# A graph network kernel in which TensorE multiplies the identity matrix beside its own work in five loops

## The chip, the cores and the metric

The kernel runs on one core of a Trainium2 chip. A core has five engines that run their own instruction streams and meet through semaphores: TensorE (matmul), VectorE, ScalarE, GpSimd (here it issues indirect DMAs) and SyncE (here it issues direct DMAs). The metric is the device time of one execution in microseconds (us).

## What is computed

Four graph networks are applied one after the other to 100000 nodes of 32 features, over 50000 edges (`src`, `dst`), each with a layer norm ahead of it and a residual:

```python
edge_index = jnp.stack([src, dst])
h = jnp.maximum(_layernorm(x, axis=-1), 0.0)
x = x + _L0_gnn_ref(h, edge_index, ...)          # softmax aggregation and an MLP
h = jnp.maximum(_layernorm(x, axis=-1), 0.0)
x = x + _L1_gnn_ref(h, ..., edge_index)          # edge MLP with batch norm
h = jnp.maximum(_layernorm(x, axis=-1), 0.0)
x = x + _L2_gnn_ref(h, edge_index, edge_attr_3, ...)
h = jnp.maximum(_layernorm(x, axis=-1), 0.0)
x = x + _L3_gnn_ref(h, edge_attr_8, ..., edge_index)
```

The change lies in the last two. `_L2_gnn_ref` is two spline convolutions, `_L3_gnn_ref` three message passing layers:

```python
# L2, twice
xW = jnp.einsum('ni,kio->nko', x, weight)
for s in range(S):
    msg = msg + basis[:, s, None] * xW[src, wi[:, s]]
out = segment_sum(msg, dst) / jnp.clip(deg, 1.0)[:, None]
h = jax.nn.elu(out + x @ root + bias)
# L3, three times
e = edge_attr @ We[l] + be[l]
msg = jax.nn.relu(x[src] + e)
h = x + segment_sum(msg, dst)
x = jax.nn.leaky_relu(h @ W[l] + b[l], negative_slope=0.01)
```

## The kernel before

Edges are sorted by destination and lie as 128 partitions x 392 columns. A stage walks over them in 49 chunks (`NCH`) of 8 columns (`CH`), that is 1024 edges, and all of a stage's loops are written out, but for those of the last stage, which are hardware loops over two chunks at a time. Nothing schedules: the order on an engine is the order in which its function issues. In each stage the engines form a pipeline over chunks.

Each stage has its own set of buffers and begins and ends with a barrier of all engines. The last part of the program, stage by stage:

- `all_nodes` works on all nodes (not over chunks).
- `conv1_edges`, the first spline stage (names `c_`): GpSimd gathers rows of nodes (8 transfers a chunk of `B.other`; in 17 of the 49 chunks 8 more of `B.own`), VectorE normalises and widens them into `c_hz` (line 1443), TensorE transposes `c_hz` in 8 pieces into two PSUM banks (line 1478), ScalarE copies these to `c_hzT` (line 1499), TensorE multiplies with the spline weights (line 1489, four products `psU` a chunk, two of them a chunk later), and VectorE weighs and sums these (lines 1453 and 1460). VectorE's third product of a chunk, `times(2)`, waits for a `psU` that stands on TensorE behind the transposes of the next chunk.
- `conv2_edges`, the first convolution: the same with gathers from a table of sums. Not changed.
- `conv3_edges`, the second convolution's end (names `c_` too): TensorE turns the features (`Turned.turn`, line 1615) and the edge attributes (`EdgeTerm.turn`, line 1759), ScalarE copies them, TensorE multiplies by `root` (line 1632) and by the edge weights (line 1772), VectorE adds the gathered sums (line 1875), applies elu, residual and norm. ScalarE copies the next chunk's transposes only after this chunk's square (`ahead(c + 1)`).
- `gin_edges`, layer 3, called for l = 0 and 1 (names `g_`): VectorE sums (line 1985), TensorE turns and multiplies, with a bias row of ones first (line 1630), ScalarE copies the result (line 1973), VectorE applies leaky relu.
- `last_edges`, the last stage (names `out_`): VectorE sums (line 2076), TensorE transposes twice (line 2058), ScalarE copies, TensorE multiplies (lines 2063, bias, and 2065, weights), ScalarE copies (line 2049), VectorE makes rows (line 2084), GpSimd scatters them, 8 transfers a chunk (line 2035).
- Between them `close_segments` runs a scan over all edges and stores a table.

GpSimd may run at most three chunks ahead of VectorE in the gathering stages (three buffers, `NR = 3`), and two behind it in the last.

Of the kernel before, what the change touches and what calls it, by code (L numbers as in the profile page):

```python
# [11 lines left out]
P = 128  # L12
# [211 lines left out]
FAKE = 100000  # L224
TOP = 3.0e38
G2, Q4 = 2, SF // P
GQ = G2 * Q4


# [1272 lines left out]
def conv1_edges(g, B, W2, W01, M, S, QB):  # L1502

    N2, NR = 2 * CH, 3
    with Phase(g, "c1") as ph:
# [5 lines left out]
        ring = [ph.sb(f"ring{i}", [P, N2, D + 1]) for i in range(NR)]  # L1511
        hd = ph.sb2("hd", [P, CH, D])
        sp_ = Spline(ph, g, W2, W01, M, 2)
        early = chosen(g, g.EARLY)
        loaded = [ph.sem(f"loaded{i}") for i in range(NR)]
        landed = [16 * CH if c in early else 16 * N2 for c in range(g.NCH)]
# [45 lines left out]
        @block.tensor  # L1562
        def _(pe):
            for c in range(g.NCH):
                sp_.turn(pe, c, 0)
                sp_.turn(pe, c, 1)
                if c:
                    sp_.multiply(pe, c - 1, (2, 3), g.spline[0])
                sp_.multiply(pe, c, (0, 1), g.spline[0])
            sp_.multiply(pe, g.NCH - 1, (2, 3), g.spline[0])  # L1570

        @block.vector
# [210 lines left out]
def conv3_edges(g, B, rows_b, M, S, QB, table):  # L1783

    N2, NR = 2 * CH, 3
    with Phase(g, "c3") as ph:
# [8 lines left out]
        x3, xc, sq = ph.sb2("x3", [P, N2, D]), ph.sb2("xc", [P, N2, D]), ph.sb("sq", [P, N2, D])  # L1795
        s, var, sd, rs = (ph.sb(n, [P, N2]) for n in ("s", "var", "sd", "rs"))
        yd, mm = ph.sb2("yd", [P, CH, D]), ph.sb("mm", [P, CH, D])
        tn, et = Turned(ph, g), EdgeTerm(ph, g, rows_b)
        block = ph.block()

        @block.gpsimd
# [36 lines left out]
        @block.tensor  # L1838
        def _(pe):
            for c in range(g.NCH):  # L1840
                pe.wait_ge(dgot[c % NR], 16 * (c // NR + 1))
                tn.turn(pe, c, halves_of(S, din[c % NR], c))
                et.turn(pe, c)
                tn.multiply(pe, c, g.root[1])
                et.multiply(pe, c, 0)

        @block.scalar
        def _(act):
# [72 lines left out]
def gin_edges(g, B, rows_b, M, S, QB, table, l):  # L1921

    N2, NR = 2 * CH, 3
    with Phase(g, f"g{l}") as ph:
        lk, summed, copied, new = ph.sem("lk"), ph.sem("summed"), ph.sem("copied"), ph.sem("new")
        got, dgot = [ph.sem(f"got{i}") for i in range(NR)], [ph.sem(f"dgot{i}") for i in range(NR)]
        kept = ph.sem2("kept")
        ring = [ph.sb(f"ring{i}", [P, CH, D]) for i in range(NR)]
        din = [ph.sb(f"din{i}", [P, CH, D]) for i in range(NR)]
        agg, e = ph.sb2("agg", [P, N2, D]), ph.sb2("e", [P, N2, D])  # L1930
        yd, mm = ph.sb2("yd", [P, CH, D]), ph.sb("mm", [P, CH, D])
        tn, et = Turned(ph, g), EdgeTerm(ph, g, rows_b)
        block = ph.block()

        @block.gpsimd
        def _(pool):
            for c in range(g.NCH):
                if c >= NR:
                    pool.wait_ge(summed, c - NR + 1)
                gather_from(g, pool, table, QB, ring[c % NR], c, 0, got[c % NR])  # L1940

        @block.sync
        def _(sp):
            def load(c):
                if c >= NR:
                    sp.wait_ge(summed, c - NR + 1)
                sp.dma_start(din[c % NR][:, :, :], lin(g, g.dst_lin, c)).then_inc(dgot[c % NR], 16)

            def store(c):
                sp.wait_ge(new, c + 1)  # L1950
                sp.dma_start(lin(g, g.dst_lin, c), yd[c % 2][:, :, :]).then_inc(kept[c % 2], 16)
            load_ahead(g, sp, NR, load, store)
            for i in range(2):
                sp.wait_ge(kept[i], 16 * ((g.NCH + 1 - i) // 2))

        @block.tensor
        def _(pe):
            for c in range(g.NCH):
                et.turn(pe, c)
                pe.wait_ge(summed, c + 1)  # L1960
                tn.turn(pe, c, [agg[c % 2][:, 4 * q:4 * q + 4, :] for q in range(4)])
                et.multiply(pe, c, l + 1)
                tn.multiply(pe, c, g.w3[l], g.bias[:, 5 + l, :])

        @block.scalar
        def _(act):
            for c in range(g.NCH):
                et.flatten(act, c)
                tn.flatten(act, c)
                act.wait_ge(tn.done, c + 1)  # L1970
                if c >= 2:
                    act.wait_ge(new, c - 1)
                act.copy(e[c % 2][:, :, :], tn.psD[c % 2][:, :].rearrange("p (t f) -> p t f", f=D)).then_inc(tn.used, 1)  # L1973

        @block.vector
        def _(v):
            link = Link(v, lk)
            for c in range(g.NCH + 1):
                if c < g.NCH:
                    cols = slice(c * CH, (c + 1) * CH)  # L1980
                    v.wait_ge(got[c % NR], 16 * CH * (c // NR + 1))
                    v.wait_ge(dgot[c % NR], 16 * (c // NR + 1))
                    if c >= 2:
                        v.wait_ge(tn.turned, c - 1)
                    link.inc(v.tensor_tensor(agg[c % 2][:, 0:CH, :], S[:, cols, :], ring[c % NR][:, :, :], ALU.add))
                    link(v.tensor_tensor(agg[c % 2][:, CH:N2, :], M[:, cols, :], din[c % NR][:, :, :], ALU.add))
                    v.sem_inc(summed, 1)
                if c:
                    k = c - 1
                    cols, b = slice(k * CH, c * CH), k % 2  # L1990
                    v.wait_ge(tn.used, c)
                    if k >= 2:
                        v.wait_ge(kept[b], 16 * (k // 2))
                    link(v.scalar_tensor_tensor(S[:, cols, :], e[b][:, 0:CH, :], 0.01, e[b][:, 0:CH, :], ALU.mult, ALU.max))  # L1994
                    v.scalar_tensor_tensor(yd[b][:, :, :], e[b][:, CH:N2, :], 0.01, e[b][:, CH:N2, :], ALU.mult, ALU.max).then_inc(new, 1)
                    et.message(v, link, k, S, M, mm)
# [7 lines left out]
def last_edges(g, B, M, out):  # L2004

    N, W = g.N, g.W
    with Phase(g, "out") as ph:
# [5 lines left out]
        agg, aT, y = ph.sb("agg", [P, CH, D]), ph.sb("aT", [P, 256]), ph.sb("y", [P, CH, D])  # L2013
        rowr, idxr = ph.sb2("rowr", [P, CH, D]), ph.sb2("idxr", [P, CH], I32)
        psA, psD = ph.ps("psA"), ph.ps("psD")
        block = ph.block()

        @block.sync
# [34 lines left out]
        def _(pe):  # L2053
            def body(k, b, first):
                c = 2 * k + b
                pe.wait_ge(zin, c + 1)
                for q in range(2):
                    ins = pe.transpose(psA[:, q * P:(q + 1) * P], agg[:, 4 * q:4 * q + 4, :].rearrange("p t f -> p (t f)"), g.ident[:, :])  # L2058
                ins.then_inc(turned, 1)
                pe.wait_ge(flat, c + 1)  # L2060
                if not (first and b == 0):
                    pe.wait_ge(leaky, c)
                pe.matmul(psD[:, 0:256], g.ones[0:1, :], over(g.bias[:, 7, :], 1, CH), start=True, stop=False, skip_group_check=True)  # L2063
                for q in range(2):
                    ins = pe.matmul(psD[:, q * P:(q + 1) * P], aT[:, q * P:(q + 1) * P], g.w3[2][:, :], start=False, stop=False, skip_group_check=True)  # L2065
                ins.then_inc(done, 1)
            chunks(g, pe, body)

        @block.vector
# [374 lines left out]
```

## Time and profile before

| | us |
|---|---|
| median of 3 runs | 9387.17 |
| lowest and highest run | 9379.37, 9951.77 |
| the profiled execution | 9400.52 |
| its span, first to last instruction | 9398.8 |
| busy in the span: TensorE matmul, weight load | 2821.1, 1768.9 |
| busy in the span: VectorE, ScalarE, GpSimd | 4174.4, 1297.4, 5190.7 |
| mean granted TensorE clock, share of full | 0.608 |

In the rows further down PE is TensorE's matmul, PEld its weight load, DVE VectorE, ACT ScalarE, POOL GpSimd. A row of the timeline has the start in the span, the time, the engine, the line in the kernel, the operation, what it writes and reads, the shape (partitions x elements), the count of instructions merged into it, and in brackets how long the engine was idle before and what ended that. Ends of matmuls are modelled. A granted clock of 0.50 is 1.2 GHz, of 1.00 2.4 GHz.

### The profile page before, as it was taken

What the parts mean: (1) busy time and instruction counts of PE and PEld (TensorE: products, weight loads), DVE (VectorE), ACT (ScalarE), POOL (GpSimd) and SP (SyncE); (2) the same over time, 40 slices, a digit from 0 to 9 for tenths busy, and PEclk for the clock granted to TensorE, in tenths of its full rate; (3) what the DMA queues carried; (4) which work ended last, traced back from release to release, by engine and by line L of the source; (5) the groups of instructions that cost most, each with busy time, mean ns of one, the idle gap of its engine ahead of it and who ended that gap; (6) DMA issues with size and microseconds to landing.
All of it is one profiled execution on the core that took longest, in us unless ns stands there. A gap on an engine that the chain in (4) does not pass through costs nothing. (4 is left out here: it accounts for less than half of the span.)

```text
span 9398.8 us, 39754 instructions
## 1 busy us (share of the span) xinstructions
PE 2821.1 (30%) x8711; PEld 1768.9 (19%) x8711; DVE 4174.4 (44%) x7182; ACT 1297.4 (14%) x2213; POOL 5190.7 (55%) x5107
## 2 busy tenths in 40 slices
PE   0000000000232310127663444277333144245222
PEld 0000000000231100003221333155222123123111
DVE  4367448970024440104543677677655411312311
ACT  0000001000011110016551000011033111011000
POOL 5744741887436637770335665266266366366366
PEclk9965555555555555558876666677655555555555
DMA  1100100001133201111111111122134222222111
GB/s 41 26 20 16 25 15 6 19 18 36 44 102 48 38 16 23 21 16 33 41 38 34 33 35 34 41 32 32 46 64 66 59 33 34 48 31 35 51 31 28
DMA packets 364620, 331.83 MB, mean 35 GB/s; under 512 B 115499, under 2 KB 339968, under 8 KB 363379
## 3 DMA queue, kind: packets, MB, share of 16 engines
q0 software_dynamic: 163072, 77.69, 9.5%
q1 hardware_dynamic: 199282, 249.37, 8.1%
q10 hardware_dynamic: 2048, 2.41, 0.1%
q8 instruction: 70, 1.15, 0.1%
q14 instruction: 148, 1.21, 0.0%
HBM read 173.11 MB, written 158.67 MB: 35 GB/s over the span
## 5 line engine op out<-in xcount | busy, mean ns | idle before, releaser
L917 POOL DMA_INDIRECT c_ring<-tab,QB x784 | 758.7, 968 | 732.2 <-POOLq L102 306.6
L917 POOL DMA_INDIRECT g_ring<-tab,QB x784 | 749.7, 956 | 621.3 <-issue 234.4
L917 POOL DMA_INDIRECT l_ring<-in_x_dram,a_own x392 | 528.6, 1348 | 386.9 <-POOLq L102 267.7
L1489 PE MATMUL c_psU<-spline,c_hzT 96*128 96x288 f32 x1568 | 547.8, 497 | 190.8 <-DVE c_V L1453 145.2
L917 POOL DMA_INDIRECT l_ring<-agg_tab,QA x392 | 393.5, 1004 | 363.3 <-POOLq L102 205.6
L917 POOL DMA_INDIRECT nodes_ring<-nodes,b_own x256 | 254.1, 993 | 594.7 <-DMA x2d_lin<-nodes_ring 516.6
L917 POOL DMA_INDIRECT H<-xe_tab,idx_a x392 | 402.1, 1026 | 320.9 <-DVEq L788 200.6
L2035 POOL DMA_INDIRECT out_dram<-out_rowr,out_idxr x392 | 386.4, 986 | 284.7 <-DVE out_idxr L2079 149.1
L917 POOL DMA_INDIRECT c_ring<-nodes,b_other x392 | 397.7, 1015 | 262.5 <-DVEq L1586 137.8
L1366 POOL DMA_INDIRECT nodes<-l1s_rowr,a_out x392 | 386.2, 985 | 264.7 <-DVE l1s_rowr L1382 145.5
L917 POOL DMA_INDIRECT sort_ring<-in_x_dram,sort_raw x392 | 402.3, 1026 | 121.3 <-issue 120.3
L917 POOL DMA_INDIRECT rows_b<-b_edges,idx_b x392 | 393.4, 1004 | 134.4 <-issue 122.8
L1994 DVE SCALAR_TENSOR_TENSOR S<-g_e 128x256 f32<-128x256 f32 x98 | 41.8, 426 | 922.7 <-ACT g_e L1973 580.3
L1453 DVE TENSOR_TENSOR c_V<-c_psU,W 128x576 f32<-128x576 f32 x392 | 286.8, 751 | 359.3 <-DMA out_dram<-nodes_o 149.2
L1460 DVE TENSOR_REDUCE M<-c_V 128x64 f32<-128x576 f32 x392 | 432.9, 1124 | 0.0
L1489 PEld LDWEIGHTS c_psU<-spline,c_hzT 96*128 96x128 f32 x1568 | 350.3, 240 | 356.8 <-issue 223.1
L1632 PE MATMUL c_psD<-root,c_aT 128*128 128x128 f32 x784 | 196.1, 429 | 526.8 <-issue 345.0
L1478 PE MATMUL c_psT<-ident,c_hz 128*96 128x128 f32 x784 | 192.7, 411 | 385.2 <-DVE c_hz L1443 292.1
L273 PE MATMUL sort_psC<-ident,sort_x 98*128 98x98 f32 (+1 forms) x148 | 30.3, 381 | 881.9 <-issue 555.1
L1632 PEld LDWEIGHTS c_psD<-root,c_aT 128*128 128x128 f32 x784 | 168.0, 316 | 567.4 <-issue 361.8
L298 DVE TENSOR_TENSOR sort_x<-sort_x 98x512 f32<-98x512 f32 (+1 forms) x315 | 189.6, 602 | 156.8 <-remote 62.1
L1630 PE MATMUL g_psD<-bias,ones 1*128 1x512 f32 x196 | 188.6, 1060 | 189.3 <-issue 188.2
(473 smaller groups left out, 8052.4 us busy)
## 6 DMA issues: line engine op xcount, KB each, us to landing
tab<-M SPq DMA_DIRECT2D x5, 6272.0 KB
nodes<-l_xout SPq DMA_DIRECT2D x40, 322.3 KB
nodes_x<-nodes SPq DMA_DIRECT2D x50, 257.8 KB
c_din<-dst_lin SPq DMA_DIRECT2D x98, 128.0 KB
c_ring<-tab,QB POOLq DMA_INDIRECT x784
dst_lin<-c_yd SPq DMA_DIRECT2D x98, 128.0 KB
g_din<-dst_lin SPq DMA_DIRECT2D x98, 128.0 KB
g_ring<-tab,QB POOLq DMA_INDIRECT x784
```

The costliest lines, as they stand in the source:

```text
L273: ins = pe.transpose(dst[:, i, 0:n], src[0:n, i // Q4, (i % Q4) * P:(i % Q4 + 1) * P], self.g.ident[0:n, 0:n])
L298: link.inc(v.tensor_tensor(lo, x, y, ALU.min))
L917: pool.indirect_dma_start(out=ring[:, at + j, :], out_offset=None, in_=table, in_offset=bass.IndirectOffsetOnAxis(ap=idx[:, w:w + 1], axis ...
L1366: pool.indirect_dma_start(out=g.nodes2, out_offset=bass.IndirectOffsetOnAxis(ap=A.out[:, w:w + 1], axis=0), in_=rowr[k % NR][:, j, :], in_ ...
L1453: v.tensor_tensor(self.V[n % 3][:, :, :, :], self.psU[i % 2][:, :, 0:288].rearrange("p t (j o) -> p t j o", o=D), over(self.W01[:, at:at + ...
L1460: v.tensor_reduce(self.M[:, at:at + 2, :], self.V[n % 3][:, :, :, :].rearrange("p t j o -> p t o j"), AX.X, ALU.add).then_inc(self.added, 1)
L1478: ins = pe.transpose(self.psT[n % self.nT][0:3 * D, t * P:(t + 1) * P], self.hz[c % 2][:, 4 * u + t, :, :].rearrange("p k f -> p (k f)"), ...
L1489: ins = pe.matmul(self.psU[i % 2][:, t, 0:288], self.hzT[c % 2][:, (2 * i + t) * P:(2 * i + t + 1) * P], w[:, :, :].rearrange("p j o -> p ...
L1630: pe.matmul(o[:, :], g.ones[0:1, :], over(bias, 1, 2 * CH), start=True, stop=False, skip_group_check=True)
L1632: ins = pe.matmul(o[:, q * P:(q + 1) * P], self.aT[c % 2][:, q * P:(q + 1) * P], w[:, :], start=bias is None, stop=bias is None, skip_grou ...
L1994: link(v.scalar_tensor_tensor(S[:, cols, :], e[b][:, 0:CH, :], 0.01, e[b][:, 0:CH, :], ALU.mult, ALU.max))
L2035: pool.indirect_dma_start(out=out, out_offset=bass.IndirectOffsetOnAxis(ap=idxr[b][:, j:j + 1], axis=0), in_=rowr[b][:, j, :], in_offset=N ...
```

## The change

A class `Spare` gives TensorE matmuls of the 128x128 identity with the identity repeated to 512 columns, into a PSUM bank of their own that nothing reads. They carry no wait and signal nothing. Per chunk there are 4 + 7 in the first spline stage, 6 + 7 in the second convolution, 5 + 6 in layer 3 (both calls), 14 in the last stage. What the kernel computes is untouched.

```diff
+class Spare:
+    def __init__(self, g, ps):
+        self.g, self.ps = g, ps
+        self.n = ps.shape[1] // P
+
+    def run(self, pe, n):
+        for i in range(n):
+            pe.matmul(self.ps.rearrange("p (t f) -> p t f", f=P), self.g.ident[:, :], over(self.g.ident[:, :], 1, self.n),
+                      start=True, stop=True)
...
@@ conv1_edges
+        spare = Spare(g, ph.ps("spare")[:, :])
...
             for c in range(g.NCH):
                 sp_.turn(pe, c, 0)
                 sp_.turn(pe, c, 1)
+                spare.run(pe, 4)
                 if c:
                     sp_.multiply(pe, c - 1, (2, 3), g.spline[0])
                 sp_.multiply(pe, c, (0, 1), g.spline[0])
+                spare.run(pe, 7)
             sp_.multiply(pe, g.NCH - 1, (2, 3), g.spline[0])
...
@@ conv3_edges
                 tn.turn(pe, c, halves_of(S, din[c % NR], c))
                 et.turn(pe, c)
+                spare.run(pe, 6)
                 tn.multiply(pe, c, g.root[1])
                 et.multiply(pe, c, 0)
+                spare.run(pe, 7)
...
@@ gin_edges
                 et.turn(pe, c)
+                spare.run(pe, 5)
                 pe.wait_ge(summed, c + 1)
                 tn.turn(pe, c, [agg[c % 2][:, 4 * q:4 * q + 4, :] for q in range(4)])
                 et.multiply(pe, c, l + 1)
                 tn.multiply(pe, c, g.w3[l], g.bias[:, 5 + l, :])
+                spare.run(pe, 6)
...
@@ last_edges
                 ins.then_inc(done, 1)
+                spare.run(pe, 14)
             chunks(g, pe, body)
```

TensorE's order in the first spline stage, at its second and third chunk, before (a call of matmul a count; `c_psT` are the transposes, `c_psU` the products; a call of line 1489 is 128x288):

```order
L1478 MATMUL c_psT<-ident,c_hz 96x128 x8
L1489 MATMUL c_psU<-spline,c_hzT 128x288 x8
L1478 MATMUL c_psT<-ident,c_hz 96x128 x8
L1489 MATMUL c_psU<-spline,c_hzT 128x288 x8
L1478 MATMUL c_psT<-ident,c_hz 96x128 x8
```

and after (line numbers are those of the changed kernel):

```order
L1493 MATMUL c_psT<-ident,c_hz 96x128 x8
L238 MATMUL c_spare<-ident 128x512 x4
L1504 MATMUL c_psU<-spline,c_hzT 128x288 x8
L238 MATMUL c_spare<-ident 128x512 x7
L1493 MATMUL c_psT<-ident,c_hz 96x128 x8
```

Between a chunk's transposes and its products now stand 4 spares, and 7 before the next transposes.

TensorE's order in the last stage's hardware loop, before, one chunk and the start of the next (`out_psA` are the transposes, `out_psD` the products):

```order
L2058 MATMUL out_psA<-ident,out_agg 128x128
L2063 MATMUL out_psD<-bias,ones 128x256 [waits sort_back,prep_mlp1]
L2065 MATMUL out_psD<-w_2,out_aT 128x128 x2
L2056 REGISTER_ALU
L2058 MATMUL out_psA<-ident,out_agg 128x128 [waits prep_blank]
```

and after:

```order
L2081 MATMUL out_psA<-ident,out_agg 128x128
L2086 MATMUL out_psD<-bias,ones 128x256 [waits sort_back,prep_mlp1]
L2088 MATMUL out_psD<-w_2,out_aT 128x128 x2
L238 MATMUL out_spare<-ident 128x512 x14
L2079 REGISTER_ALU
L2081 MATMUL out_psA<-ident,out_agg 128x128 [waits prep_blank]
```

The 14 spares stand between a chunk's products and the next chunk's transposes. (Names of semaphores in brackets are those under which their numbers were first used.)

## Rows read from the trace of the kernel before

**Rows 1.** Stretches: us; busy us (count) of PE, PEld, DVE, ACT, POOL; clock; DMA.
```profile
5050.00:5900.00 850.00, 388.38 (x1164) 264.11 (x1164) 574.43 (x872) 71.92 (x147) 518.80 (x514) 0.65 0.17 34
6772.00:7372.00 600.00, 193.37 (x735) 159.61 (x735) 309.76 (x681) 231.10 (x339) 378.39 (x392) 0.56 0.39 65
7453.00:8060.00 607.00, 284.50 (x833) 171.54 (x833) 110.38 (x294) 65.94 (x147) 375.25 (x392) 0.55 0.24 32
8164.00:8745.00 581.00, 273.41 (x809) 165.12 (x809) 107.36 (x286) 64.34 (x143) 355.22 (x372) 0.56 0.24 32
8824.00:9392.00 568.00, 149.68 (x392) 83.87 (x392) 66.09 (x196) 36.50 (x98) 386.32 (x392) 0.50 0.12 31
```

**Rows 2.** First and last start of one instruction a chunk, by line, in four stages.
```profile
L1443 DVE TENSOR_TENSOR c_hz<-S,W x49: 957/957/959, 5058.0 to 5893.1; 128x768 f32<-128x768 f32 x49
L1875 DVE TENSOR_TENSOR c_agg<-c_psD,c_ring x49: 424/424/426, 6784.0 to 7365.0; 128x256 f32<-128x256 f32 x49
L1985 DVE TENSOR_TENSOR g_agg<-S,g_ring x49: 424/426/493, 7465.2 to 8049.6; 128x256 f32<-128x256 f32 x49
L2076 DVE TENSOR_TENSOR out_agg<-M,out_din x49: 417/420/427, 8824.2 to 9363.3; 128x256 f32<-128x256 f32 x49
```

**Rows 3.** Timeline (start us, us, what) and clock: weight loads before 512-column passes.
```profile
4034.66 0.34 PEld L2215 LDWEIGHTS nodes_ps<-nodes_hT,w 128*128 128x128 f32 x1 [0.52 <-issue]
4035.51 0.34 PEld L2215 LDWEIGHTS nodes_ps<-nodes_hT,w 128*128 128x128 f32 x1 [0.52 <-issue]
...
4037.15 0.19 PEld L2215 LDWEIGHTS nodes_ps<-nodes_hT,w 128*128 128x128 f32 x1 [0.44 <-issue]
4037.58 0.19 PEld L2215 LDWEIGHTS nodes_ps<-nodes_hT,w 128*128 128x128 f32 x1 [0.24 <-issue]
...
4030.00:4036.50 6.50, 5.42 (x7) 2.32 (x8) 3.18 (x5) 2.55 (x5) 4.97 (x6) 0.50 0.09 5
4036.50:4044.00 7.50, 3.22 (x7) 0.88 (x5) 0.69 (x1) 0.69 (x1) 5.72 (x6) 0.96 0.08 5
```

**Rows 4.** Timeline: TensorE at one place of two chunks in a row, layer 3.
```profile
7718.82 0.42 PE L1759 MATMUL g_psX<-ident,rows_b 128*104 128x128 f32 x1
...
7722.81 0.27 PE L1759 MATMUL g_psX<-ident,rows_b 128*104 128x128 f32 x1
```

**Rows 5.** Timeline: the last stage's two transposes of a chunk.
```profile
9062.36 0.69 PE L2058 MATMUL out_psA<-ident,out_agg 128*128 128x128 f32 x2 [11.74 <-DVE out_agg L2076]
```

**Rows 6.** Timeline, last stage: TensorE's product and ScalarE's copy, twice.
```profile
9064.66 1.22 PE L2065 MATMUL out_psD<-w,out_aT 128*128 128x128 f32 x4
...
9065.99 0.37 ACT L2049 COPY out_r<-out_psD 128x256 f32<-128x256 f32 x1 [2.53 <-PE out_psD L2065]
...
9100.54 1.22 PE L2065 MATMUL out_psD<-w,out_aT 128*128 128x128 f32 x4
...
9114.52 0.37 ACT L2049 COPY out_r<-out_psD 128x256 f32<-128x256 f32 x1 [15.18 <-DMA g_ring<-tab,QB]
```

**Rows 7.** Timeline of GpSimd in the first convolution's loop.
```profile
6251.90 1.16 POOL L917 DMA_INDIRECT c_ring<-tab,QB  x1 [2.65 <-DVEq L1733]
...
6266.45 0.95 POOL L917 DMA_INDIRECT c_ring<-tab,QB  x1 [0.31 <-issue]
6267.70 0.95 POOL L917 DMA_INDIRECT c_ring<-tab,QB  x1 [0.30 <-issue]
```

**Rows 8.** Timeline of TensorE in one chunk, second convolution.
```profile
7071.22 2.08 PE L1632 MATMUL c_psD<-root,c_aT 128*128 128x128 f32 x8 [11.04 <-issue]
...
7074.79 0.34 PE L1759 MATMUL c_psX<-ident,rows_b 128*104 128x128 f32 x1
```

**Rows 9.** Timeline of VectorE, first spline stage: widening, first late product, next widening.
```profile
5514.47 0.96 DVE L1443 TENSOR_TENSOR c_hz<-S,W 128x768 f32<-128x768 f32 x1
...
5519.38 0.76 DVE L1453 TENSOR_TENSOR c_V<-c_psU,W 128x576 f32<-128x576 f32 x1 [1.57 <-PE c_psU L1489]
...
5528.80 0.96 DVE L1443 TENSOR_TENSOR c_hz<-S,W 128x768 f32<-128x768 f32 x1
```

More of the change, by code:

```diff
@@ L1797, in conv3_edges @@
         yd, mm = ph.sb2("yd", [P, CH, D]), ph.sb("mm", [P, CH, D])
-        tn, et = Turned(ph, g), EdgeTerm(ph, g, rows_b)
+        tn, et, spare = Turned(ph, g), EdgeTerm(ph, g, rows_b), Spare(g, ph.ps("spare")[:, :])
         block = ph.block()
@@ L1931, in gin_edges @@
         yd, mm = ph.sb2("yd", [P, CH, D]), ph.sb("mm", [P, CH, D])
-        tn, et = Turned(ph, g), EdgeTerm(ph, g, rows_b)
+        tn, et, spare = Turned(ph, g), EdgeTerm(ph, g, rows_b), Spare(g, ph.ps("spare")[:, :])
         block = ph.block()
@@ L2015, in last_edges @@
         psA, psD = ph.ps("psA"), ph.ps("psD")
+        spare = Spare(g, ph.ps("spare")[:, :])
         block = ph.block()
```

## The prediction

> **What bounds the kernel now.** I read the page first: over the span no engine is busy for more than about half the time, so shares decide nothing, and each changed stage is read by itself. The table of stretches [rows 1] shows the five changed loops over the 49 chunks of edges: the first spline stage, the second convolution, the two runs of layer 3, and the last stage. The reader is to see there that GpSimd's 8 gathers or scatters of each chunk fill about 0.61 to 0.68 of each stage, and TensorE 0.26 to 0.47 at a granted clock of 0.50 to 0.65 of full, the last stage wholly at 0.50, which is the 1.2 GHz level.
>
> A GpSimd transfer starts every 1.25 us [rows 7], so 8 need 10.0 us. The first and last chunk of each stage [rows 2] give the time of one chunk (48 steps between 49 chunks): first spline stage (5893.1-5058.0)/48 = 17.4 us, second convolution (7365.0-6784.0)/48 = 12.1, layer 3 (8049.6-7465.2)/48 = 12.2 (its second run, alike in [rows 1], is taken as equal), last stage (9363.3-8824.2)/48 = 11.2. So in the last four GpSimd is nearly the bound, 1 to 2 us short of it.
>
> The rest is a late hand-over from TensorE. [rows 6] show it: the four matmuls of line 2065 that begin at 9064.66 end 1.22 us later, and ScalarE starts at 9065.99, at once. Those at 9100.54 end at 9101.76 and ScalarE starts at 9114.52, 12.8 us late, while GpSimd issued one scatter after the other; it had to stop for it only now and then. In the first convolution, which is not changed, VectorE paces the loop and GpSimd rests 2.65 us before its next 8 gathers [rows 7]; there I found nothing late once the first chunks were through. I don't know the cause. What I use is only this: a chunk time over about 12.6 us gives GpSimd such rests, so a stage paced by TensorE should be free of most late hand-overs.
>
> **The change, priced.** One `spare` is a plain 128x128 by 128x512 matmul in f32. The nearest rows are the same shape in the stage over all nodes: there weight loads, one a 512-column pass, begin 0.85 us apart at clock 0.50 (4034.66, 4035.51) and 0.43 us apart at 0.96 (4037.15, 4037.58) [rows 3]. A plain f32 matmul is two such passes: in [rows 6] two calls of line 2065 stand as x4, and in [rows 5] two transposes as x2. So one spare is 0.86 us at the full clock and 1.71 at half. Both ends: 11 spares are 9.4 to 18.8 us, 13 are 11.2 to 22.2, 14 are 12.0 to 23.9. At the upper end TensorE would have no idle time at all in a chunk of 11 to 17 us, and [rows 3] show that a run of matmuls without a rest takes it to the upper level; I therefore take the full clock, 2.4 GHz, for all of them. The Trainium skill, page TensorE: Matmul & The Clock Gate, section Why this matters for your kernels, says to leave no longer idle gaps between bursts of matmuls, since the clock drops to half after one; by that rule alone the change would be a gain (the trace agrees on the two paces).
>
> They can be free only where they fit in TensorE's rest. They stand in program order, so everything behind them on TensorE waits.
>
> *Last stage.* Nothing of the next chunk passes the 14 spares. TensorE's own work runs from the transposes at 9062.36 over the hand-over to ScalarE to line 2065 at 9064.66 and its four passes of 0.21 [rows 5, 6]: 3.15 us at half clock. At full clock the passes lose about 1.1 of it (half of 0.43 + 0.85 + 0.85); I take 2.0. 2.0 + 12.0 = 14.0 us a chunk against 11.2: 48 x 2.8 = **+133 us**. Bounds: 13.0 (no wait between) gives +86, 15.2 gives +190.
>
> *Layer 3, twice.* Own work of a chunk from line 1759 at 7718.82 to the same line at 7722.81 [rows 4]: 4.0 us, in which the clock rose; fully at the upper level about 3.6. With 9.4: 13.0 us against 12.2, 48 x 0.8 = 40. At the start GpSimd may issue three chunks, 30 us, without a rest, a time in which hand-overs are late now too; now the chain catches up with chunks of 4 to 6 us, later it can't. I add 20. **+60 us each, +120.** Bounds +20 and +90 each.
>
> *Second convolution.* From line 1632 at 7071.22 to line 1759 at 7074.79 plus one pass [rows 8]: 3.8 us at half clock, about 2.0 at full. The wait for ScalarE's copy lies under the 6 spares. 2.0 + 11.2 = 13.2 against 12.1: 48 x 1.1 = 53, and 7 for the start: **+60 us**. Bounds +30 and +90.
>
> *First spline stage.* Here VectorE's loop counts. It widens at 5514.47, waits for the product until 5519.38 (4.9 us), and widens again at 5528.80 [rows 9]: 14.3 us a chunk where nothing is late; the mean of 17.4 comes from chunks with 16 gathers and late hand-overs. Four spares now stand between the transposes and that product: +3.4. At the full clock the 8 transposes and 4 passes lose 0.9 + 0.9, so the wait ends 1.7 later: 16.0 us. The other 7 spares (6.0 us) end before the next widening: 0.9 transposes + 3.4 + 16 passes of 0.25 (4.0) + 6.0 = 14.3 of 16.0. If all late hand-overs stay, 17.4 + 1.7: +80. If all go: 48 x (16.0-17.4) = -67. As GpSimd now rests more, but still has chunks of 16, I take **-30 us**.
>
> *All else* (first convolution, the stages between, the sort, the stage over the nodes) stands as it was; a stage's last spares end under VectorE's and the stores' tail. GpSimd, SyncE, VectorE and ScalarE get no instruction, and no wait is added: the spares' bank is their own. What queues behind them on TensorE is its next transposes and products, and ScalarE's copies and VectorE's sums wait for those.
>
> Sum: -30 + 60 + 120 + 133 = **+283 us**, on the profiled span of 9398.8 (9400.5 with what lies around it); the median of the runs is 9387, 0.14% below, so 9387 + 283 = **9670 us**, +3.0%.
>
> **Rivals.**
>
> *Evened out (0.13).* Paced by TensorE, the late hand-overs vanish in all stages and the waits between spares are shorter than I take: -67, +30, 2 x 20, +86 make +89: 9476 us. For it: the regular chunks of [rows 7]. Against: the last stage alone is above its present pace by pure passes.
>
> *The warm clock wins (0.06), on the other side.* The spares fit in the rest, TensorE's own work runs at double clock, and hand-overs come on time. TensorE is busy 388 + 193 + 285 + 273 + 150 = 1289 us in the five stages [rows 1]; at 0.5 to 0.65 a full clock would save some 500, of it perhaps half on the path: -250, 9137 us. It decides if 11 to 14 spares take less than the rest of a chunk: that needs a spare to be one pass, 0.43 us (14 = 6.0 us beside 2.0 in 11.2). The x4 for two calls speaks against it. The rule of the Trainium skill cited above (TensorE: Matmul & The Clock Gate) points this way.
>
> *Late in every chunk (0.19).* The spares' passes meet the same slowness: between 9100.54 and 9114.52 four passes took 14.0 us, and the 22 to 28 added a chunk are queued ahead of the hand-overs. If each chunk of the last four stages loses 3 us more to it, 4 x 48 x 3 = 576 more: 10246 us; with 1 us, 9862. GpSimd's rest of 3 us a chunk speaks against, as it does in the first convolution; runs of 16 gathers in the first spline stage for it.
>
> **How the numbers follow.** My forecast has 0.62, its own range 9575 to 9780 by the bounds of its terms. The range to hold 8 in 10 runs from 9500, inside the evened-out case, to 9950, inside the late one. A measurement here can tell 2% (188 us) from no change: slower means over 9575. Slower: 0.60 of the forecast, and 0.19 of the last, and a little of the evened-out case, 0.82; same 0.13; faster 0.05.
>
> **What would show it.** In the profile after, the spare line should stand with 2 x (49 x 11 + 49 x 13 + 2 x 49 x 11 + 49 x 14) = 5880 passes of 0.43 us pitch, the granted clock near 1.0 in the five stages, the last stage's chunks 14.0 us apart, layer 3's 13.0, the second convolution's 13.2 and the first spline stage's about 16.5, and GpSimd resting 3 to 4 us after each 8. The forecast is wrong if the clock stays near 0.5 (then the chunks would be 20 us and over, and the time over 11,000 us), if spares are single passes, or if ScalarE's copies start many microseconds after TensorE's last pass in most chunks.

## The result, and the profile after

The changed kernel takes 9851.99 us (median of 4, 9849.09 to 9863.49) where the kernel before takes 9387.17. (That is the median of three runs; a fourth, at 9951.77, was in a slower state of the chip and is left out of the ratio.) The ratio is 1.0495, with a 95% interval of 1.0474 to 1.0515: 465 us, 4.9% slower. The prediction said 9670 us, +283: right in direction, 182 us too low.

The page of the changed kernel first. The lines are its row of granted clock over 40 equal slices, and its three groups of spare passes (count | busy us, mean ns | idle before):

```profile
PEclk9975555555655655578779897776998898899999
...
L238 PE MATMUL c_spare<-ident 128*128 128x512 f32 x2352 | 1062.6, 601 | 14.2 <-issue 12.4
L238 PE MATMUL g_spare<-ident 128*128 128x512 f32 x2156 | 961.5, 597 | 0.0
...
L238 PE MATMUL out_spare<-ident 128*128 128x512 f32 x1372 | 598.7, 594 | 0.0
```

2352 + 2156 + 1372 = 5880 passes: a spare is two passes, as priced. The table of stretches of the changed kernel (the columns of [rows 1]), for the first spline stage, the second convolution, layer 3 twice and the last stage:

```profile
5039.00:5986.00 947.00, 752.34 (x2189) 399.64 (x2190) 561.34 (x857) 67.42 (x144) 524.18 (x511) 0.89 0.15 30
6888.00:7536.00 648.00, 626.67 (x1963) 322.33 (x1962) 302.83 (x666) 231.83 (x333) 374.53 (x383) 0.98 0.34 58
7637.00:8280.00 643.00, 594.70 (x1815) 287.86 (x1816) 105.29 (x282) 67.34 (x140) 361.46 (x383) 0.96 0.22 29
8399.00:9042.00 643.00, 594.17 (x1816) 287.85 (x1817) 105.97 (x285) 67.34 (x140) 361.57 (x383) 0.96 0.22 29
9151.00:9817.00 666.00, 643.79 (x1703) 297.19 (x1704) 62.26 (x191) 35.76 (x96) 370.18 (x376) 0.99 0.10 26
```

The clock, between 0.50 and 0.65 in [rows 1], is now between 0.89 and 0.99, and TensorE fills 92 to 97% of the last four stages. The first and last start of one instruction a chunk, to be set against [rows 2]; for the first spline stage I take a reduction of its normalization, of which all 49 are recorded, and show that row of the kernel before (L1582) too:

```profile
L1582 DVE TENSOR_REDUCE c_ln_s<-c_ring x49: 668/674/695, 5053.4 to 5888.5; 128x16 f32<-128x512 f32 x49
```

```profile
L1600 DVE TENSOR_REDUCE c_ln_s<-c_ring x49: 667/674/687, 5038.8 to 5985.8; 128x16 f32<-128x512 f32 x49
L1895 DVE TENSOR_TENSOR c_agg<-c_psD,c_ring x49: 424/425/427, 6887.8 to 7536.4; 128x256 f32<-128x256 f32 x49
L2007 DVE TENSOR_TENSOR g_agg<-S,g_ring x49: 425/426/427, 7636.6 to 8280.4; 128x256 f32<-128x256 f32 x49
L2007 DVE TENSOR_TENSOR g_agg<-S,g_ring x49: 424/426/427, 8398.9 to 9042.0; 128x256 f32<-128x256 f32 x49
L2100 DVE TENSOR_TENSOR out_agg<-M,out_din x49: 416/419/427, 9150.6 to 9817.2; 128x256 f32<-128x256 f32 x49
```

From these rows the 450 us between the two profiled spans (9398.8 and 9848.8) can be placed:

| where | before, us | after, us | change | forecast |
|---|---|---|---|---|
| first spline stage | 835.1 | 947.0 | +112 | -30 |
| second convolution | 581.0 | 648.6 | +68 | +60 |
| layer 3, both runs | 584.4 + 585.5 | 643.8 + 643.1 | +117 | +120 |
| last stage | 539.1 | 666.6 | +128 | +133 |
| between the stages, the end, and all ahead of the first spline stage | | | +26 | 0 |

In the last line +41 lie between the stages and at the end, of which 18 and 20 us stand behind the two runs of layer 3 (8280.4 to 8398.9 is 118.5 us, where it was 100.7), and -15 ahead of the first spline stage. Three lines of the sum hold within 8 us. One, the first spline stage, has the wrong sign.

The timeline of the first spline stage in the changed kernel shows what it waits for. The product (line 1504, 8 passes) begins at 5573.93, at full pace, and ends 2.10 us later; VectorE, which waits for it in line 1468, begins at 5584.51, 8.5 us late. ScalarE's two copies, whose transposes stand ahead of that product on TensorE, begin 4.2 us apart. GpSimd issued one transfer after the other up to 5580.65; VectorE moves 2.9 us after that one's end:

```profile
5573.93 2.10 PE L1504 MATMUL c_psU<-spline,c_hzT 96*128 96x288 f32 x8
...
5574.70 0.58 ACT L1514 COPY c_hzT<-c_psT 96x512 f32<-96x512 f32 x1 [7.26 <-DMA rows_b<-b_edges,idx_b]
...
5578.86 0.58 ACT L1514 COPY c_hzT<-c_psT 96x512 f32<-96x512 f32 x1 [3.58 <-DMA rows_b<-b_edges,idx_b]
...
5580.65 0.95 POOL L932 DMA_INDIRECT c_ring<-nodes,b_other  x1 [0.30 <-issue]
5584.51 0.76 DVE L1468 TENSOR_TENSOR c_V<-c_psU,W 128x576 f32<-128x576 f32 x1 [12.61 <-DMA out_dram<-nodes_o]
```

So the late hand-overs of [rows 6] were still there, once in every three chunks: chunks of 15.7, 17.2 and 25.1 us, 58.1 together. They had even become a little more frequent: of the stage's 48 chunks 12 took over 20 us before, and 16 do now.

### The profile page after: what moved, and what is told of

Read it like the earlier page. It is cut to its first block and busy times, and to the rows that moved or that the text cites. A ratio compares the mean times of both kernels' runs of the same rounds, so it can differ in the third digit from the quotient of the medians.

```text
span 9848.8 us, 51514 instructions
## 1 busy us (share of the span) xinstructions
PE 4866.1 (49%) x14591; PEld 2574.0 (26%) x14591; DVE 4169.0 (42%) x7182; ACT 1306.9 (13%) x2213; POOL 5200.6 (53%) x5107
## 5 line engine op out<-in xcount | busy, mean ns | idle before, releaser
L238 PE MATMUL c_spare<-ident 128*128 128x512 f32 x2352 | 1062.6, 601 | 14.2 <-issue 12.4
L238 PE MATMUL g_spare<-ident 128*128 128x512 f32 x2156 | 961.5, 597 | 0.0
L238 PE MATMUL out_spare<-ident 128*128 128x512 f32 x1372 | 598.7, 594 | 0.0
L1504 PE MATMUL c_psU<-spline,c_hzT 96*128 96x288 f32 x1568 | 490.6, 453 | 189.2 <-DVE c_V L1468 155.2
L238 PEld LDWEIGHTS c_spare<-ident 128*128 128x128 f32 x2352 | 448.8, 194 | 507.4 <-issue 496.6
L238 PEld LDWEIGHTS g_spare<-ident 128*128 128x128 f32 x2156 | 398.5, 192 | 456.1 <-issue 456.1
L1504 PEld LDWEIGHTS c_psU<-spline,c_hzT 96*128 96x128 f32 x1568 | 313.0, 212 | 358.6 <-issue 273.4
```

The source lines that it names most:

```text
L238: pe.matmul(self.ps.rearrange("p (t f) -> p t f", f=P), self.g.ident[:, :], over(self.g.ident[:, :], 1, self.n), start=True, stop=True)
L1504: ins = pe.matmul(self.psU[i % 2][:, t, 0:288], self.hzT[c % 2][:, (2 * i + t) * P:(2 * i + t + 1) * P], w[:, :, :].rearrange("p j o -> p ...
```

## Experiments

**All experiments ran later, on four chips,** and on each of them the kernel before takes 7812 to 7826 us, not 9387. Ratios are always to the kernel before on the same chip, run beside it, and what differs from the first pair is itself a finding (below).

### The first spline stage alone, and its cause

`spline_only` keeps the 4 and 7 spares of the first spline stage and drops all others:

```
                 et.turn(pe, c)
-                spare.run(pe, 6)
...
                 et.multiply(pe, c, 0)
-                spare.run(pe, 7)
...
-                spare.run(pe, 5)
...
-                spare.run(pe, 6)
...
-                spare.run(pe, 14)
```

> The 4 and 7 spares of the first spline stage alone; the other three stages as in the kernel before. In the changed kernel that stage went from 17.4 to 19.7 us a chunk (line 1600 from 5038.8 to 5985.8, against 835.1 before). Theory A (the cost belongs to the stage itself): it takes 947 us again, and the whole kernel about 9395 + 112 + 6 - 15 = 9500 us, 1.1% over before, all other stages at their times of before. Theory B (stages act on each other, so that the stages' differences don't add): the stage stays near 835 to 860 us when the later ones have no spares, and the time is within 0.4% of before.

Ratio 1.0093 (1.0063 to 1.0123). The stage took 756 us, 15.75 a chunk, not 947:

```profile
L1600 DVE TENSOR_REDUCE c_ln_s<-c_ring x49: 671/674/689, 4019.5 to 4775.6; 128x16 f32<-128x512 f32 x49
```

The expectation had both theories start from 835 us, and the stage before is 680 us where nothing is late (next section), so neither number fits. What is left of theory A is that the stage costs +76 us by itself, without any other stage's spares; with all of them in place it takes the same 756 (`after_again`, below). It does not settle what made +112 of it in the first pair.

`before_early49` and `after_early49` move the second set of 8 gathers of the remaining 17 chunks into the stage over all nodes, in the kernel before and in the changed one:

```
-    g.PICKED, g.EARLY = 24, 32
+    g.PICKED, g.EARLY = 24, 49
```

> The same move of gathers in the kernel before, without spares. Theory F: no late hand-overs, 14.3 us a chunk instead of 17.4: 686 us instead of 835; with 0 to 170 us more in the stage over the nodes the kernel takes 9245 to 9420. Theory G: 17.4 us a chunk stay, 835 us, 9395 to 9565.

> The changed kernel, with the second set of 8 gathers of all 49 chunks (not of 32) moved ahead, into the stage over all nodes: the first spline stage then has 8 gathers in every chunk. Theory F (the late hand-overs there come with GpSimd's long runs of transfers, 8 + 16 + 8): they go, and the stage takes the 16.0 us a chunk that the prediction worked out, 770 us instead of 947. Theory G (the spares' places alone give 19.7 us a chunk): it stays over 900 us. The stage over the nodes has 17 x 8 x 1.25 = 170 us more of GpSimd's work, beside pauses of GpSimd of 30 us each: 0 to 170 us longer. By F 9680 to 9850, by G 9850 to 10020.

Measured: 1.0120 (1.0090 to 1.0150) and 1.0980 (1.0950 to 1.1011). The first spline stage took 670.9 us without and 753.7 with spares:

```profile
L1582 DVE TENSOR_REDUCE c_ln_s<-c_ring x49: 666/674/690, 4100.9 to 4771.7; 128x16 f32<-128x512 f32 x49
```

```profile
L1600 DVE TENSOR_REDUCE c_ln_s<-c_ring x49: 671/674/681, 4118.6 to 4872.3; 128x16 f32<-128x512 f32 x49
```

14.0 and 15.7 us a chunk are close to theory F's 14.3 and 16.0. But `spline_only` reached 15.75 with its runs of 16 gathers in place, so the two runs don't show that the runs of gathers made hand-overs late: here nothing was late with or without them. The moved gathers cost about 106 us in the stage over the nodes (the first spline stage starts at 4100.9 in place of 3994.9).

### The same pair again, where nothing is late

> The kernel before once more, for its trace beside the runs of this call (in the runs before this one it took 7821 us, and GpSimd's 8 transfers a chunk took 10.0 us in layer 3, without a pause). Theory H (the missing 1570 us against the first trace are hand-overs from TensorE that are no longer late): the stages that GpSimd paces take 10.0 to 10.2 us a chunk, the first spline stage 14.0, the sort 1062 us instead of 1514. Theory I (everything runs quicker by one factor, as by a quicker clock): single operations such as line 1453's reduction or a gather are shorter by 17%.

> The changed kernel beside it. Where no hand-over is late, the spares meet chunks of 10.0 us: first spline stage 15.75 against 14.0 us a chunk (+85), second convolution 13.0 against 10.2 (+134), layer 3 12.55 against 10.0 twice (+245), last stage 13.9 against 10.12 (+181), ends of stages +35 to 45: 8490 to 8530 us where before takes 7821, a ratio of 1.085 to 1.09. If late hand-overs are back, the ratio is near 1.05 as in the first pair.

The kernel before took 7805 us in one run. The changed one has ratio 1.0866 (1.0835 to 1.0898), 8502 us against 7815. First and last starts in the kernel before (first spline stage, second convolution, layer 3's first run, last stage):

```profile
L1582 DVE TENSOR_REDUCE c_ln_s<-c_ring x49: 666/673/687, 3994.9 to 4674.9; 128x16 f32<-128x512 f32 x49
L1875 DVE TENSOR_TENSOR c_agg<-c_psD,c_ring x49: 423/425/426, 5540.3 to 6032.3; 128x256 f32<-128x256 f32 x49
L1985 DVE TENSOR_TENSOR g_agg<-S,g_ring x49: 424/426/427, 6132.5 to 6612.2; 128x256 f32<-128x256 f32 x49
L2076 DVE TENSOR_TENSOR out_agg<-M,out_din x49: 415/420/427, 7282.3 to 7768.2; 128x256 f32<-128x256 f32 x49
```

and the same four places in the changed kernel:

```profile
L1600 DVE TENSOR_REDUCE c_ln_s<-c_ring x49: 666/674/697, 4016.9 to 4772.5; 128x16 f32<-128x512 f32 x49
L1895 DVE TENSOR_TENSOR c_agg<-c_psD,c_ring x49: 424/425/425, 5645.1 to 6269.8; 128x256 f32<-128x256 f32 x49
L2007 DVE TENSOR_TENSOR g_agg<-S,g_ring x49: 424/425/427, 6369.8 to 6973.2; 128x256 f32<-128x256 f32 x49
L2100 DVE TENSOR_TENSOR out_agg<-M,out_din x49: 415/420/426, 7802.3 to 8469.5; 128x256 f32<-128x256 f32 x49
```

Theory H holds and I falls: operations have the durations of the first trace (424 to 427 ns for the additions above, as in [rows 2]); what is gone are waits. The timeline of the last stage in the kernel before shows it: TensorE's product at 7500.84 ends at 7502.06 and ScalarE starts at 7502.17, while GpSimd issues scatter after scatter, 1.29 us apart, without a rest. In the first trace the same sequence gave 12.8 us of delay [rows 6]:

```profile
7500.84 1.22 PE L2065 MATMUL out_psD<-w,out_aT 128*128 128x128 f32 x4
7501.07 0.98 POOL L2035 DMA_INDIRECT out_dram<-out_rowr,out_idxr  x1 [0.30 <-issue]
7502.17 0.37 ACT L2049 COPY out_r<-out_psD 128x256 f32<-128x256 f32 x1 [2.53 <-PE out_psD L2065]
7502.36 0.98 POOL L2035 DMA_INDIRECT out_dram<-out_rowr,out_idxr  x1 [0.30 <-issue]
```

Time of a chunk in us, all from such rows divided by 48; "late" is the first pair less the second:

| stage | before, first pair | after, first pair | before again | after again | late before | late after |
|---|---|---|---|---|---|---|
| first spline stage | 17.40 | 19.73 | 14.17 | 15.74 | 3.2 | 4.0 |
| second convolution | 12.10 | 13.51 | 10.25 | 13.01 | 1.9 | 0.5 |
| layer 3 (first run) | 12.18 | 13.41 | 9.99 | 12.57 | 2.2 | 0.8 |
| last stage | 11.23 | 13.89 | 10.12 | 13.90 | 1.1 | 0.0 |

This table explains the size of the result. Where nothing is late, the spares cost 48 x (1.57 + 2.76 + 2 x 2.57 + 3.78) = 636 us in the five loops, since in the last four GpSimd's 10 us a chunk are then the bound that TensorE has to stay under. In the first pair they cost 424, as TensorE's own pace gave back 212 us of late time. It gave it back wherever the loop is TensorE's, and in the first spline stage it did not. Behind the two runs of layer 3 another 19 and 18 us are lost here (6973.2 to 7091.4 in place of 6612.2 to 6711.9 for the first), as in the first pair.

What is left of late time in the changed kernel's later stages lies at their start. In the first pair the third chunk of each run of layer 3 takes 42.5 and 42.3 us, where it takes 9.7 and 10.0 on the later chip, and the first chunk of the second convolution 34.0 in place of 12.1; no later chunk of these stages is over 15.0.

### Which spares of the first spline stage cost

`spline_ahead` keeps only the 4 spares between the transposes and the product, `spline_behind` only the 7 behind it, and `all_behind` has 11 behind it; no other stage has any. The edits, in the stage's loop of the changed kernel:

```
spline_ahead:                        spline_behind:                      all_behind:
                                     -                spare.run(pe, 4)   -                spare.run(pe, 4)
-                spare.run(pe, 7)                                        -                spare.run(pe, 7)
                                                                         +                spare.run(pe, 11)
```

> Only the 4 spares between the transposes and the first product of the first spline stage. Theory J (VectorE's loop waits for that product, the others are hidden, as the prediction worked out: +3.4 for the spares, -1.7 for the quicker clock): 15.5 to 15.8 us a chunk, the whole cost of the 11, +80 us. Theory K (TensorE as a whole is the bound, 11 spares count alike): 14.3 to 14.7 us a chunk, +20 to +35 us. If the clock falls with fewer spares, the 4 cost up to 6.8: over 17 us a chunk, +145 us or more.

> Only the 7 spares behind the product. Theory J: hidden in TensorE's rest, 13.7 to 14.0 us a chunk, and the whole kernel within 15 us of before (6 spares there took 13.78). Theory K: 14.8 to 15.3 us a chunk, +40 to +60 us.

> All 11 spares of the first spline stage stand behind the product, none ahead of it; none in the other stages. So far, without late hand-overs: no spare 14.0 to 14.2 us a chunk, 7 behind 13.8, 4 ahead 17.0, 4 ahead and 7 behind 15.7. Theory J (what counts is whether VectorE waits for a product behind the spares): TensorE's own work at full clock is 4.9 us a chunk and 11 spares 9.5, 14.4 together, so 14.3 to 14.6 us a chunk, +10 to +25 us. Theory K (the number counts, not the place): 15.7 again, +75 us.

| kernel | ratio (interval) | us a chunk | clock in the stage |
|---|---|---|---|
| none | 1 | 14.17 | 0.72 |
| 4 ahead | 1.0186 (1.0160 to 1.0212) | 17.00 | 0.80 |
| 7 behind | 0.9988 (0.9976 to 1.0000) | 13.78 | 0.95 |
| 4 ahead, 7 behind | 1.0093 (1.0063 to 1.0123) | 15.75 | 0.99 |
| 11 behind | 1.0062 (1.0041 to 1.0083) | 15.13 | 0.99 |

The clock of the fourth line is from `after_again`. In VectorE's timeline, widening (the first line of each pair) and the first product that VectorE has to wait for after it, for no spares, 4 and 7, and 4 ahead alone:

```profile
4510.25 0.96 DVE L1443 TENSOR_TENSOR c_hz<-S,W 128x768 f32<-128x768 f32 x1
...
4515.17 0.76 DVE L1453 TENSOR_TENSOR c_V<-c_psU,W 128x576 f32<-128x576 f32 x1 [1.58 <-PE c_psU L1489]
```

```profile
4509.26 0.96 DVE L1458 TENSOR_TENSOR c_hz<-S,W 128x768 f32<-128x768 f32 x1
...
4515.79 0.76 DVE L1468 TENSOR_TENSOR c_V<-c_psU,W 128x576 f32<-128x576 f32 x1 [3.19 <-PE c_psU L1504]
```

```profile
4510.28 0.96 DVE L1458 TENSOR_TENSOR c_hz<-S,W 128x768 f32<-128x768 f32 x1
...
4518.19 0.76 DVE L1468 TENSOR_TENSOR c_V<-c_psU,W 128x576 f32<-128x576 f32 x1 [4.56 <-PE c_psU L1504]
```

4.9, 6.5 and 7.9 us. The prediction had 4.9 + 3.4 - 1.7 = 6.6 for the second, so theory J's mechanism stands in these three: what delays VectorE is what lies ahead of the product. But the 4 alone are dearer than all 11. The stretches of one such chunk, TensorE's rest, then transposes and first spares, then the remaining spares and products, show why:

```profile
4504.60:4511.20 6.60, 0.34 (x2) 0.00 (x0) 5.91 (x13) 0.31 (x1) 5.08 (x6) 0.70 0.14 18
4511.20:4514.40 3.20, 3.11 (x10) 2.32 (x11) 2.42 (x4) 1.16 (x2) 2.59 (x3) 0.54 0.52 127
4514.40:4521.00 6.60, 6.10 (x20) 3.39 (x19) 2.81 (x4) 0.00 (x0) 4.87 (x6) 1.00 0.13 13
```

After 6.6 us in which it did next to nothing TensorE stands at the lower level when the transposes come, and they and the first spare go at half pace. The 7 behind had kept it at the upper one. I had expected 15.5 to 15.8 there, or over 17 if the clock fell; it fell, and the chunk takes 17.0.

`all_behind` came out at 15.13, between J (14.3 to 14.6) and K (15.7). Its row for the stage gives TensorE 695 of 726 us busy:

```profile
4015.00:4741.00 726.00, 695.08 (x2180) 374.98 (x2181) 561.43 (x856) 66.03 (x144) 500.19 (x511) 0.99 0.20 39
```

TensorE is the bound. Its chunk is 11 spares, 9.5 us, and 5.7 us of its own, with waits for VectorE to free a product's buffer among them; I had counted 4.9. VectorE waits 6.0 us for its product there, not 3.3 as with 7 behind: once TensorE is the bound, spares behind a chunk's products delay the next chunk's.

### Do spares that fit pay?

`fitting` has 0 and 6, 4 and 5, 4 and 4, and 9 spares; `narrow` has all the spares of the changed kernel with 128 columns in place of 512:

```
fitting (the last stage; the other counts likewise):
-                spare.run(pe, 14)
+                spare.run(pe, 9)
narrow:
-        spare = Spare(g, ph.ps("spare")[:, :])
+        spare = Spare(g, ph.ps("spare")[:, 0:P])
```

> Fewer spares, so many that they fit into TensorE's rest by 0.86 us each: 0 and 6 in the first spline stage, 4 and 5 in the second convolution, 4 and 4 in layer 3, 9 in the last stage (own work 2.0 to 3.6 us a chunk, so 9.7 to 10.5 of 11.2 to 12.2). Theory C (the spares cost only what does not fit): within 1% of before, 9300 to 9490. Theory D (the warm clock wins where spares fit): TensorE's clock is near 0.9 in these stages, its own work and hand-overs are quicker by 1 us a chunk, and the time is 200 us or more lower, under 9200. Theory E (each spare adds to late hand-overs, also where it fits): 9600 and over.

> The changed kernel with all its spares in their places, each of 128 instead of 512 columns. Theory L (a spare costs its columns): two passes of 0.11 us at the full clock, 0.22 us each, so 2.4 us a chunk for 11 and 3.1 for 14: all but the 4 ahead of the product fit, layer 3 and the last stage stay at 10.0 to 10.2 us a chunk, and the kernel is within 1% of before. If the clock stays at the lower level in those stages, 0.43 us each: the first spline stage +1.7 a chunk, +80 us, the rest still as before. Theory M (a spare costs a fixed time for its instruction and weights): 12 us a chunk and more in layer 3, over 3% slower. Theory D (a warm clock wins): under 7700 where before takes 7820.

`fitting`: 1.0030 (1.0013 to 1.0048). `narrow`: 1.0075 (1.0058 to 1.0092). Stretches of the first spline stage, the second convolution, layer 3's first run and the last stage, for the kernel before and for `fitting`:

```profile
3995.00:4675.00 680.00, 351.12 (x1144) 249.43 (x1144) 565.36 (x858) 70.59 (x144) 503.40 (x511) 0.72 0.21 42
5542.00:6034.00 492.00, 188.03 (x715) 156.18 (x715) 303.88 (x667) 226.40 (x334) 371.34 (x382) 0.56 0.46 76
6134.00:6614.00 480.00, 297.41 (x820) 173.87 (x819) 106.92 (x287) 64.16 (x144) 359.94 (x382) 0.50 0.30 39
7283.00:7769.00 486.00, 146.95 (x386) 82.42 (x385) 64.13 (x191) 35.71 (x96) 363.61 (x371) 0.50 0.14 35
```

```profile
3996.00:4657.50 661.50, 529.45 (x1711) 301.55 (x1712) 561.88 (x858) 67.68 (x144) 498.63 (x511) 0.94 0.21 43
5530.00:6020.00 490.00, 465.79 (x1571) 243.68 (x1570) 301.48 (x661) 225.78 (x332) 371.43 (x380) 1.00 0.47 77
6120.00:6605.00 485.00, 472.78 (x1543) 233.90 (x1544) 107.20 (x286) 67.34 (x140) 365.25 (x383) 0.99 0.30 39
7315.00:7800.00 485.00, 455.03 (x1249) 209.44 (x1247) 64.48 (x190) 35.76 (x96) 366.33 (x373) 0.99 0.13 35
```

In the second convolution and the last stage the spares do fit. The clock went from 0.56 and 0.50 to 1.00 and 0.99, and from first to last chunk the stages take 493.7 us (before 492.0) and 488.2 (485.9): theory C. GpSimd's 8 transfers are the bound at about 10 us a chunk, and a quicker TensorE has nothing to give. The Trainium skill, page TensorE: Matmul & The Clock Gate, section Why this matters for your kernels, is right about the clock here and says nothing of the time of such a stage.

In layer 3 they don't quite fit. The count was made for chunks of 12.2 us, and here GpSimd's take 10.0. TensorE has no rest, and a chunk of it takes 10.3 us:

```profile
7159.80 0.27 PE L1776 MATMUL g_psX<-ident,rows_b 128*104 128x128 f32 x1
...
7170.10 0.27 PE L1776 MATMUL g_psX<-ident,rows_b 128*104 128x128 f32 x1
```

The stage as VectorE sees it grows by only 4 us, from 480 to 484, since TensorE falls behind it: ScalarE's last copy of a product comes 18.4 us after VectorE's last addition, where it was 6.9. That is paid behind each of the two runs, 11.5 and 11.4 us. With 8 us within the runs, and against 18.6 us won in the first spline stage, it is more than half of the 21 us by which `fitting` is longer (spans of 7825.1 and 7803.6).

In `narrow` the second convolution, layer 3 and the last stage stayed at 10.2, 10.0 and 10.1 us a chunk, with the clock between 0.74 and 0.79, and only the first spline stage grew, to 15.3. There VectorE's wait for the product is 5.6 to 6.6 us in place of 4.9, by the four narrow spares ahead of it: theory L, with 1.1 us a chunk between the 0.9 and 1.7 that it allows. Theory E, on late hand-overs, could not be tested where none is late. A spare costs its columns.

### A version a little faster than both

In `spline_behind` VectorE's first product came 3.3 us after the widening in the median, instead of 4.9, and still the stage fell only by 18 us, to 661.5. The trace before has 528 gathers in that stage, 660 us at 1.25. `behind_early38` moves 6 more sets of 8 gathers out of it:

```
                 sp_.turn(pe, c, 1)
-                spare.run(pe, 4)
...
-    g.PICKED, g.EARLY = 24, 32
+    g.PICKED, g.EARLY = 24, 38
```

with the 7 behind kept and no spares elsewhere.

> The 7 spares behind the product alone took 661.5 us in the first spline stage, and 528 gathers at 1.25 us are 660: GpSimd had become its bound, while single chunks there already showed 12.5 us. Here 6 more chunks have their second 8 gathers moved into the stage over the nodes, 480 gathers stay, 600 us. Theory N (the warm clock's gain was hidden by GpSimd): the stage falls to 600 to 615 us, 65 to 80 under before; the stage over the nodes grows by 6 x 6.2 = 37 us (17 chunks cost 106 there), and the kernel is 0.3 to 0.6% faster than before. Theory O (VectorE's own loop takes 13.8 with the warm clock): the stage stays at 655 to 665 us, and the kernel is 0.2 to 0.5% slower than before.

Ratio 0.9945 (0.9926 to 0.9963), 7781 us against 7812; the stage took 614 us, as theory N has it:

```profile
L1599 DVE TENSOR_REDUCE c_ln_s<-c_ring x49: 667/677/701, 4033.9 to 4648.0; 128x16 f32<-128x512 f32 x49
```

It is 0.5% faster than the kernel before, a small gain, but the interval leaves out 1. The moved gathers alone don't give it: with all 17 sets moved and no spares the stage still took 670.9 us (`before_early49`). It was run only where nothing is late.

## Why the prediction came out as it did

- **A spare is two passes of 0.43 us, 0.86 together.** Right: 5880 passes, and the last stage's 28 lie between 9506.98 and the next chunk's transposes at 9519.00, 0.43 us each (timeline of TensorE in the changed kernel):

```profile
9504.96 0.38 PE L2081 MATMUL out_psA<-ident,out_agg 128*128 128x128 f32 x2
...
9506.98 12.18 PE L238 MATMUL out_spare<-ident 128*128 128x512 f32 x28
9519.00 0.38 PE L2081 MATMUL out_psA<-ident,out_agg 128*128 128x128 f32 x2
```

- **Last stage, 2.0 + 12.0 = 14.0 us a chunk, +133.** Right: 13.9 in both pairs, and +128 in the first.
- **Layer 3, 13.0 a chunk and 20 us for the start, +60 each.** Right in the stage, +59 and +58, and for the reason given: chunks take 12.9 us once the start is over, and the third, 42.5 us where it was 35.8 before, is no longer caught up. The stage's end was priced at nothing, and 18 and 20 us more lie behind it: VectorE's last addition no longer marks the end of TensorE's work. In the second run it starts at 9042.0, and ScalarE's last copy of a product (line 1995) at 9065.5, 23.5 us later; before, these stood at 8735.8 and 8741.0.
- **Second convolution, 13.2, +60.** 13.5, +68; 13.0 a chunk once the start is over.
- **First spline stage, -30: the term that failed.** The price of the spares was right. Where nothing is late the stage takes 15.74 us a chunk, as against the 16.0 worked out, and the wait for the product 6.5 as against 6.6. Wrong was the other half, that part of the late hand-overs would go because GpSimd rests more. They stayed, 4.0 us a chunk instead of 3.2, and the stage took 19.7 us a chunk. The case that the text priced at +80, "all late hand-overs stay", is what happened, and at +112 it went beyond that bound: 76 us for the spares, as priced, and 36 of late time more, where the forecast counted on about 110 less. This term alone accounts for 142 of the missing 167 us between forecast and profiled spans. Why hand-overs are late, and why GpSimd's rests did not end that here, stays open.
- **"A chunk time over about 12.6 us gives GpSimd such rests, so most late hand-overs go."** It held where TensorE paces the loop (late time of 1.1 to 2.2 us a chunk fell to 0.0 to 0.8, and that lies at the stages' start), and not in the first spline stage with its 16 gathers in a row. As a rule on the cause it falls: on the later chips GpSimd issues without a rest through all of layer 3 (480 us for 48 x 8 transfers of 1.25) and nothing is late.
- **"Evened out", 0.13.** Its first half came true in the last four stages, where late hand-overs went once the start was over; in the first spline stage they stayed, and the last stage's chunks are not shorter than priced.
- **"Warm clock wins", 0.06.** Rightly low. Its condition, a spare of one pass, is false, and where spares did fit the clock rose and nothing was won: it wins only where TensorE is waited for. That is the product of the first spline stage (4.9 to 3.3 us), and even there GpSimd's 528 gathers take most of the gain.
- **The ranges.** The forecast's own range, 9575 to 9780, did not hold 9852. It was called that of the terms' bounds, but these add up to +89 to +540, 9476 to 9927, which would have. The wide range, 9500 to 9950, held it by the case "late in every chunk", though not by that rival's mechanism: the late time did not grow in the last four stages. That the rival's figure for 1 us a chunk, 9862, lies so near the result is luck.

## What to carry to other kernels

In this kernel filler matmuls were free only in a stage where TensorE's own work plus the filler stayed under the pace of the engine that bounds it (10.3 against 10.0 us a chunk already cost 11 us at each end), and they paid only where somebody waited for TensorE, placed behind the product that is waited for and not ahead of it. Work out each stage's bound without its stalls before pricing an addition: a stall that happens to cover the addition, or one that you hope it removes, is not a property of the kernel, and the same edit was worth 4.9% with and 8.7% without them.

## What the runs showed that I had not expected

- The same kernel took 9387 us in the first pair and 7805 to 7826 on the four later chips, with equal durations of single operations. From its first to its last instruction the sort took 1514 us and 1061, the stage over the nodes about 1100 and 735. What differs are signals between engines that arrive late in the first pair's traces, 12.8 us for one of TensorE's in [rows 6] and more at the start of a stage: in the changed kernel's layer 3 four transposes end at 7654.64, and ScalarE, idle for 15.88 us, copies them at 7692.24. What makes them late stayed open, and the chip itself is a possible cause that nothing here tests: no later run had any, so nothing could be tried against them. Long runs of GpSimd's transfers go with them in the first pair but are not enough to make them.
- Adding work can cheapen work: 4 spares alone cost 2.8 us a chunk, all 11 together 1.6, as the clock was then at the upper level when the chunk began.
